# Last stage of a graph network: destination rows by plain loads, output loop on two sets of PSUM banks

## What is computed

```python
def _L3_gnn_ref(x, edge_index, edge_attr, Wl, bl, Wn, bn):
    e_proj = edge_attr @ Wl + bl
    msg = relu(x[src] + e_proj)
    agg = segment_sum(msg, dst, num_segments=x.shape[0])
    return (x + agg) @ Wn + bn
...
x = layernorm(x + _L3_gnn_ref(x, edge_index, edge_attr_64, Wl, bl, Wn, bn))
```

## Time and profile before

| | us |
|---|---|
| median of 3 runs | 4035.1 (4032.59 to 4035.59) |
| profiled execution | 4035.14, of which the span of the trace is 4033.3 |
| granted TensorE clock, mean over the span | 0.551 |

### The profile page before, as it was taken

The page is one execution under the profiler, slowest core; times in us unless marked ns, Lnnn a source line. Parts: engine busy times, 40 slices in busy tenths (PEclk is TensorE's granted clock), DMA queues, the critical chain, the costliest instruction groups (busy, mean ns, idle before and its releaser), DMA issues. The chain is left out here.

```text
span 4033.3 us, 34837 instructions
## 1 busy us (share of the span) xinstructions
PE 1601.3 (40%) x5666; PEld 1320.0 (33%) x5666; DVE 2409.5 (60%) x5486; ACT 1239.6 (31%) x3433; POOL 2499.7 (62%) x2420
## 2 busy tenths in 40 slices
PE   1988989977122156512552000000000277065221
PEld 1888888866122135301220000000000166054221
DVE  5565565549885977678985333348854234443554
ACT  1555555542232255402552222210000144033110
POOL 5777777777701774057602777770377677776777
PEclk9555555555555555556776555555555566566555
DMA  2555556655101244224642555540000155344000
GB/s 56 166 168 165 166 168 184 189 166 141 39 28 34 55 123 128 79 61 112 176 138 84 155 150 150 155 126 0 5 20 20 54 160 158 99 131 115 16 18 17
DMA packets 255330, 421.00 MB, mean 104 GB/s; under 512 B 79304, under 2 KB 86746, under 8 KB 255244
## 3 DMA queue, kind: packets, MB, share of 16 engines
q1 hardware_dynamic: 177932, 348.51, 28.0%
q0 software_dynamic: 77312, 71.64, 9.0%
HBM read 185.35 MB, written 236.81 MB: 105 GB/s over the span
## 5 line engine op out<-in xcount | busy, mean ns | idle before, releaser
L577 PE MATMUL banks<-node_w,x_t 65*125 65x200 f32 x1600 | 551.6, 536 | 0.0
L577 PEld LDWEIGHTS banks<-node_w,x_t 65*125 65x125 f32 x1600 | 514.9, 330 | 4.1
L224 POOL DMA_INDIRECT edge_rows<-x_rows,norm_s x400 | 413.9, 1035 | 144.8 <-issue 125.0
L790 PE MATMUL banks<-ident,cross_in 125*65 125x125 f32 (+4 forms) x26 | 11.2, 430 | 1236.4 <-DVE cross_in L813 848.0
L790 PEld LDWEIGHTS banks<-ident,cross_in 125*65 125x65 f32 (+4 forms) x26 | 3.9, 150 | 1242.1 <-DVE cross_in L813 850.4
L240 POOL DMA_INDIRECT x_rows<-r_x,src_scat_i x200 | 222.1, 1110 | 125.4 <-DVE r_x L2028 63.4
L240 POOL DMA_INDIRECT out_dram<-n_out,scat_i x200 | 222.5, 1112 | 80.1 <-issue 62.0
L620 DVE TENSOR_REDUCE n_var<-n_sq 125x8 f32<-125x512 f32 x125 | 85.6, 686 | 306.4 <-ACT n_sq L634 306.4
L224 POOL DMA_INDIRECT tops<-norm_rows,src_i x200 | 202.6, 1013 | 71.6 <-issue 68.8
L224 POOL DMA_INDIRECT edge_rows<-x_rows,key_i x200 | 199.0, 995 | 77.2 <-issue 60.7
L240 POOL DMA_INDIRECT norm_rows<-edge_rows,scat_i x200 | 205.4, 1027 | 66.6 <-issue 63.3
(11 more groups left out here) (455 smaller groups left out, 5230.2 us busy)
## 6 DMA issues: line engine op xcount, KB each, us to landing
h_rows<-r_h SPq DMA_DIRECT2D x125, 462.0 KB
x_rows<-r_x SPq DMA_DIRECT2D x125, 241.5 KB
x_rows<-r_x SPq DMA_DIRECT2D x125, 224.0 KB
r_x<-x_rows SPq DMA_DIRECT2D x125, 224.0 KB
x_rows<-n_out SPq DMA_DIRECT2D x125, 224.0 KB
n_in<-in_x_dram SPq DMA_DIRECT2D x100, 224.0 KB
x_mixed_edge_rows<-e_dup SPq DMA_DIRECT2D x50, 448.0 KB
n_c<-x_rows SPq DMA_DIRECT2D x100, 224.0 KB
```

The costliest lines, as they stand in the source:

```text
L224: g.indirect_dma_start(out=to[:, j, :], out_offset=None, in_=table, in_offset=bass.IndirectOffsetOnAxis(ap=idx[:, j:j + 1], axis=0)).then_ ...
L577: done = pe.matmul(product[h][:, n // 2, n % 2, :], x_t[u][:, at:at + P], node_w[:, :], start=True, stop=True)
L790: pe.transpose(crossings["bank"][0:cols, 0:rows], frm, ident[0:rows, 0:rows]).then_inc(s_tout, 1)
```

## The change

The 200 gathers of destination rows are dropped; `xd` is filled by plain loads of the first 25,000 rows of X3, in six groups of columns (`edges_dma`). The source gathers signal by the same six groups (`gather_groups`). EP is loaded by the same groups into `xd` ahead of the destination rows, two groups at a time, and a message is now one add and one relu over a whole group (32 to 40 columns, the last 16), done in place in `xs`.

The output loop is one loop over 50 pairs with two sets of buffers: loads alternate between `n_c` and `n_in`, stores between `n_out` and `r_x2`, product banks between 1, 2 and 3, 4, and the copy out of them between the two halves of `e_dup`. PE's wait on `so.copied` is now for the pair two back. ACT handles the products of pair i-1 before it copies the transposes of pair i. A load is waited for by the transposes two pairs back, a store is issued three pairs behind the load.

On DVE the messages are set between pairs of the loop: after pair 8, 18, 28, 38, 44 and 46. A quarter of the scans comes before pair 46, another quarter before pair 48, the rest after the loop. SP issues the X3 and EP loads of a group between the loop's loads at pairs 12, 22, 32 and 42.

```diff
-def skewed(eng, pairs_n, body):
+def skewed_by_two(eng, pairs_n, body):
...
-        OUT_SPLIT = NPAIRS * 3 // 5
-        outs = ((0, OUT_SPLIT), (OUT_SPLIT, NPAIRS))
...
+        o_in, o_out = (n_c, n_in), (n_out, r_x2)
...
+        def out_load(sp, i, q):
+            for u in range(U):
+                if not is_first(i) and not is_at(i, 1):
+                    sp.wait_ge(so.turned, 2 * i - 3 + u)
+                rows_dma(sp, flat(o_in[q][u][:, :, :]), node_rows(X3[EDGES:ROWS], i, u, D), so_loaded[q][u])
...
+        def out_sp(sp, start, end):
+            with nc.sync.Fori(start // 2, end // 2) as k:
+                for q in range(2):
+                    out_load(sp, 2 * k + q, q)
+                    out_store(sp, 2 * k + q - 3, 1 - q)
...
-                        if not is_at(i, 1):
-                            pe.wait_ge(so.copied, 2 * i - 3 + u)
-                        add_bias(pe, bank[2 + u][0:P, :], wn_bias[:, :])
+                        if not is_at(i, 1) and not is_at(i, 2):
+                            pe.wait_ge(so.copied, 2 * i - 5 + u)
+                        add_bias(pe, y_bank(1 - q, u), wn_bias[:, :])
...
+        OUT_CUTS = (8, 18, 28, 38, 44, 46)
+
+        def edges_dma(sp, to, table, n, done):
+
+            rows = table[0:EDGES].rearrange("(p j) f -> p j f", p=P)
+            cols = slice(groups[n][0] * NC, groups[n][1] * NC)
+            for part in (slice(0, SPLIT), slice(SPLIT, P)):
+                sp.dma_start(to[part, cols, :], rows[part, cols, :]).then_inc(done, 16)
...
+                edges_dma(sp, xd, EP, 0, s4.loaded[0])
+                for i in range(2):
+                    out_load(sp, i, i)
+                edges_dma(sp, xd, EP, 1, s4.loaded[1])
...
+                    if n:
+                        sp.wait_ge(s4.msg, n)
+                        edges_dma(sp, xd, X3, n - 1, s4.own)
+                        edges_dma(sp, xd, EP, n + 1, s4.loaded[(n + 1) % 2])
+                    out_sp(sp, start, end)
...
-                gather(g, xs_all, X3, src_place_i_all, s4.gathered)
-                gather(g, xd_all, X3, dst_place_i_all, s4.gathered_dst)
-                for part in outs:
-                    out_stored(g, part)
+                gather_groups(g, xs_all, X3, src_place_i_all)
+                out_stored(g)
...
+                def message(n):
+                    cols = slice(groups[n][0] * NC, groups[n][1] * NC)
+                    dve.wait_ge(s_got[n], got_done(n, 6))
+                    dve.wait_ge(s4.loaded[n % 2], ROWS_DONE * (n // 2 + 1))
+                    v.link(dve.tensor_tensor(xs[:, cols, :], xs[:, cols, :], xd[:, cols, :], ALU.add))
+                    dve.tensor_scalar(xs[:, cols, :], xs[:, cols, :], 0.0, None, ALU.max).then_inc(s4.msg, 1)
+
+                for n, (start, end) in enumerate(zip((0, *OUT_CUTS), OUT_CUTS)):
+                    out_dve(dve, start, end)
+                    message(n)
+                dve.wait_ge(s4.msg, len(groups))
+                scan_rows_dve(dve, xs, range(0, D // 4))
+                out_dve(dve, OUT_CUTS[-1], NPAIRS - 2)
+                scan_rows_dve(dve, xs, range(D // 4, D // 2))
+                out_dve(dve, NPAIRS - 2, NPAIRS)
+                scan_rows_dve(dve, xs, range(D // 2, D))
+                carry_dve(dve, xs[:, J - 1, :], D, "sum", carry_rows[0][:, :])
```

More of the change, by code:

```diff
@@ L672, in out_stored @@
[L672 to L679, removed]
+        so = phase("out", "turned turned_sb y squares copied var dev row", "loaded0 loaded1 stored0 stored1")
+        so_loaded, so_stored = (so.loaded0, so.loaded1), (so.stored0, so.stored1)
+        o_in, o_out = (n_c, n_in), (n_out, r_x2)
+        assert NPAIRS % 2 == 0
@@ L691, in body, with out_act @@
                     for u in range(U):
-                        pe.wait_ge(so.loaded[u], ROWS_DONE * i + ROWS_DONE)
+                        pe.wait_ge(so_loaded[q][u], ROWS_DONE // 2 * (i - q) + ROWS_DONE)
                         for c in range(NC // 2):
-                            done = pe.transpose(bank[6 + u][:, c * P:(c + 1) * P], flat(n_c[u][:, 2 * c:2 * c + 2, :]), ident[0:P, 0:P])
+                            done = pe.transpose(bank[5 + u][:, c * P:(c + 1) * P], flat(o_in[q][u][:, 2 * c:2 * c + 2, :]), ident[0:P, 0:P])
                         done.then_inc(so.turned, 1)
[L696 to L701, removed]
+            skewed_by_two(nc.tensor, NPAIRS, body)
+        def out_act(act):
+            def body(i, q, a, b):
+                if b:
+                    for u in range(U):
+                        act.wait_ge(so.y, 2 * i - 1 + u)
+                        nc.scalar.activation(flat(n_sq[u][:, :, :]), y_bank(1 - q, u), ACT.Square, scale=D ** -0.5).then_inc(so.squares, 1)
+                        if not is_at(i, 1) and not is_at(i, 2):
+                            act.wait_ge(so.row, 2 * i - 5 + u)
+                        nc.scalar.copy(e_dup[u][:, :, 1 - q, :], cols3(y_bank(1 - q, u))).then_inc(so.copied, 1)
                 if a:
@@ L704, in body @@
                         act.wait_ge(so.turned, 2 * i + u + 1)
-                        if b:
-                            act.wait_ge(so.y, 2 * i - 1 + u)
-                        nc.scalar.copy(n_t[u][:, :], bank[6 + u][:, 0:NC // 2 * P]).then_inc(so.turned_sb, 1)
+                        nc.scalar.copy(n_t[u][:, :], bank[5 + u][:, 0:NC // 2 * P]).then_inc(so.turned_sb, 1)
                 if b:
[L709 to L714, removed]
                     for u in range(U):
@@ L1961, in build @@
         s3 = phase("cos", "norms roots logits exps centred squares var dev x3", "scattered")
+        s3.done_turns = 0
         xr, xc = rows_of(0, D), rows_of(J * D, D)
```

137 lines of the change are left out of this document (63 added, 74 removed).

## The result

| | us | ratio to before |
|---|---|---|
| before, median of 4 | 4033.85 (4032.0 to 4035.59) | |
| changed kernel, median of 4 | 3849.48 (3839.53 to 3865.51) | 0.9549, 95% interval 0.9514 to 0.9583 |
| forecast | 3884 (3835 to 3940) | |

The gain is 184 us where 151 were forecast. The profiled execution took 3840.28 us, at the quick end of the four, with a span of 3838.4.

The account below looks back on a forecast made before the run. POOL's gathers bound the stage, the output loop ending only 23 us before them. Loop, messages, scans and queued loads (15 + 15 + 5), then scans and carry put the final loop at 3572.3, 151.2 us earlier: 3884 us, range 3835 to 3940.

Parts of the forecast that it names:

- Destination gathers: 200 gathers of 1.35 us, 270 us, leave POOL, free from about 3453; the output loop becomes the bound.
- Start: The output loop's first reduction comes 1.5 us later, at 3212.4, as EP's first group goes ahead of the first loads.
- Slot: Time per pair in the output loop: 7.05 us slow, 4.7 fast, 6.2 taken as the mix, against 7.57 before.
- Messages: Six messages on DVE within the output loop cost about 22 us, 1.5 of each hidden: 15 taken, ends 4 and 22.
- Scans in the loop: Two blocks of 16 scans on DVE, before pairs 46 and 48, 8.9 us each less 1.5 hidden: 15 us.
- Queued bursts: At four places 2.56 MB of X3 and EP stand ahead of the next pair's load: 5 us, ends 0 and 20.
- The end: Behind 48 pairs of the output loop: last pair 3.5 us, then 4.0 from its first reduction to its last row.
- Double buffered loads: Output loop's loads issued about 1.5 slots ahead: worth nothing by itself, since no transpose waited before; cover for queued loads.
- the two rivals on the clock: PE's clock in the output loop stays at 0.50: 3925 us, chance 0.16; or stays up: 3834 us, chance 0.13.
- The rival in which the clock stays up: PE holds full clock in the output loop; DMAs at 228 GB/s decide, 50 us earlier: 3834 us, chance 0.13.
- Slower: The DMAs don't hold the output loop's mixed traffic, under 139 GB/s; at 130, 4067 us; chance 0.02.
- The interludes are not covered: Messages, scans and queued loads stop the output loop at full price, 60 us instead of 35, plus refills: 3933, chance 0.11.

Follow-up runs that it names:

- e2: The changed kernel with the 200 destination gathers put back on POOL, each group behind its message, instead of plain loads: 4043.21 us, ratio 1.0013.
- e1: The changed kernel with one set of product banks again, keeping ACT's new order (transposes copied last): 3844.43 us, ratio 0.9526.
- e5: The changed kernel with both sets of product banks, but ACT's old order (transposes copied first): 3865.06 us, ratio 0.9576.
- e6: The changed kernel with one set of load buffers, a load issued after the transposes of the pair just before: 3887.8 us, ratio 0.9622.

## Why the prediction was right, point by point

The time, 3849.48, is 35 us below the forecast and within its range. The start of the final loop in the profiled execution, 3529.3 instead of 3572.3, is 43.0 us early; that execution is 9.2 us quicker than the median. By the steps of the sum, with the profiled execution's numbers:

- *Destination gathers*: right. 270 us leave POOL, the last gather is at 3458.3 (forecast about 3453), the scatters follow as before, and e2 shows that nothing comes without this step.
- *Start*: 3205.40 instead of 3212.4. Of these 7.0, 2.8 lie ahead of the stage (its first gather is at 3187.9, not 3190.7); the loads being there early gave 5.5 - 2.8 = 2.7 against the loop before and not a loss of 1.5.
- *Slot*: 6.2 forecast. Without messages (3.9), stops (9.6) and scans (5.1), 281.5 / 49 = 5.74, 22 us over 48 slots. The two widths were right, 7.01 for 7.05 and 4.63 for 4.7; the share of fast slots was the term that was off, (7.01 - 5.74) / 2.38 = 53% instead of 36. The banks were named as what removes the wait; e1 shows that with ACT's order they aren't needed, and e5 that without it they do it as well. The formula for `n_t` was ACT's order all along.
- *Messages*: 3.9 instead of 15. Their own work was sized right, 21.7 for 22 us. In a slow slot, where DVE works less than 4 of 7.01 us, a message showed nothing (slot 30, 7.01 us); in a fast slot 0.75 to 1.56 showed. The 1.5 us of cover taken for each was too little. Not in this term, nor in the forecast, is that the clock can fall behind the longer pause; that part of the price lies in the share of fast slots. That ACT and PE run ahead on work of two pairs, so that one slot's delay need not reach PE, is how I read it; no run isolates it.
- *Scans in the loop*: 5.1 instead of 15 by this count, slot 48 with 12.09 instead of 7.01. The second block shows behind slot 49, 3.4 us of it, and stands in the term of the end; together 8.5.
- *Queued bursts*: 9.6 instead of 5, two stops of 4.1 and 5.5 us over a slow slot. The place and the kind were named. The four bursts aren't 2.56 MB each but 2.30, 2.56, 2.30 and 1.79, by the groups of 32 to 40 and 16 columns; the first two stopped PE for 6.25 and 7.73 us in fast slots, the third came among slow slots and lengthened one by 0.15 us, the fourth cost a wait of 2.07 us.
- *The end*: from slot 49 to the last row, and one slot, 11.7 instead of 3.5 + 4.0, of which 3.4 is the second block of scans. Scans and carry 17.9 instead of 19.8: the diff's `scan_rows_dve` links once per call and not behind every second scan, which I read over, 15.82 / 32 = 0.494 us each instead of 0.557.

Together 7.0 + 22 + 11 + 10 - 4.6 - 4.2 + 1.9 = 43.

Nearly all of these errors are shares and covers that had been guessed, and most of them go one way; that the sum stayed within 35 us owes something to the terms that went the other way, 8.8 us. *Double buffered loads are worth nothing by themselves, they are cover for what follows* is borne out as far as e6 goes: with one set the fast slot keeps its 4.63 us, and the cover was worth some 30 us, for which the sum had no term of its own. An argument around the sum fell: the two rivals on the clock were weighed with the node stage's 0.50 at a busy PE. The same stretch of the changed kernel:

```profile
700.00:750.00 50.00, 44.22 (x151) 42.03 (x152) 30.69 (x65) 28.42 (x79) 38.41 (x39) 1.00 0.64 190
```

It is recorded at 1.00 here, while that stage's 1600 matmuls have the same median of 537 ns, and last from 89.5 to 876.9 in one profile and from 90.6 to 878.8 in the other. So the recorded clock of that stage says nothing of this loop, where record and slot width do go together (1.00 with 4.63, 0.50 with 7.01). The rival in which the clock stays up should have had more than its 0.13: with about half of the slots fast the result lies 15 us from its 3834. What kept the forecast near is that both its widths were worked out per clock state, so that only the mix was a guess.

*Slower* had its point at 139 GB/s; the loop drew up to 262 at a share of 0.95. *The interludes are not covered* was right for the loads, right in part for the scans, and wrong for the messages' own time.

## What to carry to other kernels

Ask of each wait which other edit of the same change would remove it too: here two edits each removed it, and only undoing both shows what they are worth. A removed bound is worth what the next one leaves, and the order of the bounds has to be written out (here: gathers, 270 us; then the loop; 27 us below, the source gathers). And put bulk loads on a shared queue between the small loads and stores that someone waits for, never in one piece ahead of them: moving 12 issues took this kernel from 0.9549 to 0.9488 of the kernel before.

## What the hardware showed unexpectedly

PE busy without a pause isn't enough for the full clock: up to 50.00 of 50 us at 0.50 in this loop. The opposite also holds, 18 slots with a pause of 0.87 us in each at 1.00. What came ahead of every fall of the clock in these loops was one pause of PE of 1.57 us or more, and a message of VectorE was enough for it. A shorter slot can therefore lose: e5's is 0.07 to 0.47 us shorter in each state, and its loop 27 us longer than the changed kernel's in the profiled executions. The 16 DMA engines took loads, stores and gathers together at 262 GB/s over 25 us, with gathers over the whole loop at a mean interval of (3458.3 - 3187.9) / 200 = 1.35 us, where the old loop left them 1.31.
